# Recurrent layer of a twelve-layer network: a quarter of the product with B on GpSimd, step sizes computed once

## The reference, cut to what matters

```python
xz = x @ in_proj_w.T + in_proj_b
x_main, z = jnp.split(xz, 2, axis=-1)
xc = silu(causal_conv(x_main, conv_w) + conv_b)          # 4 taps, per channel
ssm = xc @ x_proj_w.T + x_proj_b                         # 33 columns
B_param, C_param = ssm[..., :16], ssm[..., 16:32]
delta = softplus(ssm[..., -1:])                          # one step size per position
A = -exp(A_log)                                          # 256 x 16
h = exp(A * dt) * h + dt * B_t * x_t                     # over 512 positions, per channel and state
y = sum over states of h * C_t + D * x_t
y = (y * silu(z)) @ out_proj_w.T + out_proj_b
out = layernorm(y + x) * gamma + beta
```

## Time and profile before

| | us |
|---|---|
| three timed runs | 2643.38, 2636.57, 2642.61 |
| their median | 2642.61 |
| profiled execution, its time | 2648.85 |
| its span, first to last instruction | 2647.0 |
| busy: TensorE, VectorE, ScalarE, GpSimd | 2102.6, 1704.8, 1021.6, 495.3 |
| mean granted TensorE clock, share of full speed | 0.867 |

### The profile page before, as it was taken

One profiled execution on the slowest core, in us unless ns is written; L12 is line 12 of the kernel. 1 busy time (PEld: TensorE's weight loads), 2 busy tenths in 40 slices (PEclk: granted clock), 3 DMA queues, 4 the chain that ended last, 5 costly groups with the idle time before them and its releaser, 6 DMA issues. The chain is left out here.

```text
span 2647.0 us, 35471 instructions
## 1 busy us (share of the span) xinstructions
PE 2102.6 (79%) x11888; PEld 1380.2 (52%) x11912; DVE 1704.8 (64%) x4085; ACT 1021.6 (39%) x2225; POOL 495.3 (19%) x843
## 2 busy tenths in 40 slices
PE   6696999976997895547774996597599869988788
PEld 3453888853554444112222454486333346766677
DVE  5565677764675556789997455456689665655655
ACT  2353222211564451444441343321177723443333
POOL 0331111001111420226662331010211000000000
PEclk8597999986897797679997798799699879999989
DMA  8320000003111310000001320001311010000000
GB/s 314 98 57 13 1 1 1 1 24 96 49 49 36 96 45 0 0 0 0 0 0 63 95 44 13 0 1 42 119 41 43 23 40 1 0 0 0 0 1 17
DMA packets 60046, 94.41 MB, mean 36 GB/s; under 512 B 11312, under 2 KB 33136, under 8 KB 58736
## 3 DMA queue, kind: packets, MB, share of 16 engines
q1 hardware_dynamic: 29792, 55.57, 6.2%
q0 software_dynamic: 29952, 36.45, 5.7%
q10 hardware_dynamic: 144, 0.39, 0.1%
HBM read 65.63 MB, written 31.29 MB: 37 GB/s over the span
## 5 line engine op out<-in xcount | busy, mean ns | idle before, releaser
L904 DVE TENSOR_REDUCE m<-banks 128x1 f32<-128x512 f32 (+3 forms) x512 | 272.6, 584 | 80.1 <-PE banks L1057 53.5
L2435 PEld LDWEIGHTS banks<-w_ffn,eh 128*128 128x128 f32 x2144 | 280.1, 191 | 21.7
L2435 PE MATMUL banks<-w_ffn,eh 128*128 128x128 f32 x2144 | 281.7, 275 | 0.0
L1325 DVE TENSOR_REDUCE m<-banks 128x2 f32<-128x308 f32 x384 | 164.3, 475 | 173.2 <-PE banks L1604 97.2
L1025 ACT ACTIVATE p<-banks 128x512 f32<-128x512 f32 (+3 forms) x512 | 233.7, 522 | 97.0 <-PE banks L1103 56.6
L2423 PE MATMUL banks<-x_hi,w_hi 128*128 128x512 f32 x472 | 211.7, 448 | 18.7 <-PEq L330 18.7
L1055 PE MATMUL banks<-K,Qf 32*128 32x512 f32 (+2 forms) x512 | 181.1, 511 | 38.1 <-PEq L330 33.2
L2425 PE MATMUL banks<-x_hi,w_lo 128*128 128x512 f32 x472 | 188.7, 400 | 0.0
L2424 PE MATMUL banks<-x_lo,w_hi 128*128 128x512 f32 x472 | 188.0, 398 | 0.0
L2405 ACT ACTIVATE et<-banks 128x512 f32<-128x512 f32 x140 | 83.7, 598 | 248.5 <-PE banks L2425 198.2
L2715 POOL TENSOR_TENSOR hc<-sh,cb 128x1024 f32<-128x1024 f32 x64 | 153.1, 2393 | 113.6 <-ACT cb L2730 108.0
(11 more groups left out here) (398 smaller groups left out, 4293.1 us busy)
## 6 DMA issues: line engine op xcount, KB each, us to landing
Qf<-stack_q_plain POOLq DMA_DIRECT2D x48, 256.0 KB, 3.0
Qf<-stack_q_masked POOLq DMA_DIRECT2D x32, 256.0 KB, 3.0
K<-stack_k_self POOLq DMA_DIRECT2D x32, 256.0 KB, 3.1
w_ffn<-ffn_dram SPq DMA_DIRECT2D x1, 6144.0 KB, 35.7
stack_q_plain<-q_hi SPq DMA_DIRECT2D x24, 256.0 KB, 3.5
stack_q_masked<-q_hi SPq DMA_DIRECT2D x16, 256.0 KB, 2.9
stack_k_self<-k_hi SPq DMA_DIRECT2D x16, 256.0 KB, 3.1
K<-stack_k_ctx POOLq DMA_DIRECT2D x48, 80.0 KB, 2.6
```

What stands on the lines that cost most here:

```text
L904: ins = dve.reduce_max(k.m[:, t, h:h + 1], bank[:, 0:(t + 1) * P if k.kind == "page" else S], AX)
L1325: dve.reduce_max(k.m[:, t:t + 2, h], first_banks[c % 3][:].rearrange("p (a k) -> p a k", a=2)[:, :, 0:S2], AX).then_inc(sem("max_done"), 1)
L2435: last = pe.matmul(bank[:, t * P:(t + 1) * P], k.h[:, n % RING, t * P:(t + 1) * P], w(down.format(e))[:, i * P:(i + 1) * P], start=(i == 0 ...
```

## The change

In the scan, VectorE makes only the first 384 of the 512 columns of each half of `dbx`. ScalarE copies the last 128 columns of B from PSUM to SBUF (`bb`), after its copy of C of the step before, and GpSimd multiplies `dtx` by that copy, ahead of its multiplication by C of the step before. VectorE now waits for the copy (`bb_ready`) before its part of `dbx`, and for GpSimd's part (`rest_dbx`) before the scans. `dtx` has two buffers and is made for the next batch at s = 8.

In the inputs, the step size argument is formed with the positions along the partitions: per batch four times two matmuls with `xc` as the stationary operand and one column of weights, all batches into 16 columns of one bank. B and C of batch b go to rows 32 b to 32 b + 31 of one bank. After the last batch, the softplus chain runs once on 128 x 16 and the split once on 128 x 512; ScalarE copies the parts to their places in `k.bc` (twelve copies of 32 x 512); VectorE makes diagonal matrices of the step sizes, TensorE multiplies them by a matrix of ones (16 matmuls of 128 x 128), and ScalarE copies the result to `k.dt`. The bodies of the removed `split`, `step_sizes` and `logarithms` (lines 2510 to 2535 and 2587 to 2593 of the kernel before) are left out:

```diff
--- before.py
+++ after.py
@@ -126,7 +126,7 @@
-    "m_xp_b": (1, lambda i: i["L2_attn_x_proj_b"][0:32].reshape(32, 1)),
+    "m_xp_b": (1, lambda i: np.tile(i["L2_attn_x_proj_b"][0:32].reshape(32, 1), (4, 1))),
@@ -2447,6 +2447,7 @@
+OWN = 384
@@ -2463,7 +2464,8 @@
-        self.dtx = sb("dtx", [P, 2, S])
+        self.dtx = sb("dtx", [P, 2, 2, S])
+        self.bb = sb("bb", [P, 2, S])
@@ -2478,17 +2480,19 @@
-    bf, bh = sb("bf", [32, S]), sb("bh", [32, S], BF16)
-    raw, e, ln, d, iz = (sb(name, [P, S]) for name in ("raw", "e", "ln", "d", "iz"))
+    bf, parts = sb("bf", [P, S]), sb("bparts", [P, 3, S], BF16)
+    raw, e, ln, d, iz, dt = (sb(name, [P, B * QT]) for name in ("raw", "e", "ln", "d", "iz", "dtp"))
+    diag = sb("diag", [P, 2, QT, P])
+    bc_bank, dt_bank = ps[4], ps[5]
-            dve.memset(k.bc[:], 0.0)
+            dve.memset(k.bc[96:P, :], 0.0)
@@ -2507,43 +2511,38 @@
-            def split(b):
...
-            def step_sizes(b):
...
             convolve(0)
...
             for b in range(B):
...
                 if b + 1 < B:
+                    convolve(b + 1)
+                activate(b)
+
+            dve.wait_ge(sem("dt_done"), B)
+            ch.link(dve.tensor_scalar(raw[:], dt_bank[:, 0:B * QT], w("m_dt_b"), None, ALU.add))
+            dve.scalar_tensor_tensor(e[:], raw[:], -1.0, raw[:], ALU.mult, ALU.max).then_inc(sem("abs_ready"), 1)
+
+            dve.wait_ge(sem("bc_done"), B)
+            ch.link(dve.tensor_scalar(bf[:], bc_bank[:], w("m_xp_b"), None, ALU.add))
+            for part in range(3):
+                dve.tensor_copy(parts[:, part], bf[:]).then_inc(sem("part_ready"), 1)
+                dve.wait_ge(sem("part_ready"), part + 1)
+                if part < 2:
+                    ch.link(dve.tensor_tensor(bf[:], bf[:], parts[:, part], ALU.subtract))
+
+            dve.wait_ge(sem("log_ready"), 1)
+            ch.link(dve.tensor_scalar(iz[:], d[:], -1.0, 0.0, ALU.add, ALU.is_equal))
+            ch.link(dve.scalar_tensor_tensor(d[:], d[:], -1.0, iz[:], ALU.add, ALU.add))
+            ch.link(dve.reciprocal(d[:], d[:]))
+            dve.tensor_tensor(ln[:], ln[:], iz[:], ALU.add)
+            ch.link(dve.tensor_tensor(d[:], d[:], e[:], ALU.mult))
+            ch.link(dve.tensor_tensor(d[:], d[:], ln[:], ALU.mult))
+            ch.link(dve.scalar_tensor_tensor(dt[:], raw[:], 0.0, d[:], ALU.max, ALU.add))
+            for b in range(B):
+                if b >= 2:
+
+                    dve.wait_ge(sem("spread_done"), b - 1)
+                dve.tensor_tensor(diag[:, b % 2], over(w("ident"), 1, QT), over(dt[:, b * QT:(b + 1) * QT], 2, P), ALU.mult).then_inc(sem("diag_ready"), 1)
+            dve.wait_ge(sem("diag_ready"), B)
@@ -2584,26 +2583,33 @@
-            def logarithms(b):
...
             act.wait_ge(sem("halved"), 1)
             first_tap(0)
...
             for b in range(B):
...
+                gate(b)
+                if b == 0:
+                    first_tap(1)
+                activate(b)
                 if b + 2 < B:
                     first_tap(b + 2)
+
+            act.wait_ge(sem("abs_ready"), 1)
+            nc.scalar.activation(e[:], e[:], ACT.Exp, scale=-1.0).then_inc(sem("e_ready"), 1)
+            act.wait_ge(sem("e_ready"), 1)
+            nc.scalar.activation(d[:], e[:], ACT.Identity, bias=1.0).then_inc(sem("e1_ready"), 1)
+            act.wait_ge(sem("e1_ready"), 1)
+            nc.scalar.activation(ln[:], d[:], ACT.Ln).then_inc(sem("log_ready"), 1)
+
+            for part in range(3):
+                act.wait_ge(sem("part_ready"), part + 1)
+                for b in range(B):
+                    last = nc.scalar.copy(k.bc[32 * part:32 * part + 32, b * S:(b + 1) * S], parts[32 * b:32 * b + 32, part])
+                last.then_inc(sem("part_placed"), 1)
+            for b in range(B):
+                act.wait_ge(sem("spread_done"), b + 1)
+                nc.scalar.copy(k.dt[:, b], ps[b][:]).then_inc(sem("dt_ready"), 1)
+            act.wait_ge(sem("dt_ready"), B)
+            act.wait_ge(sem("part_placed"), 3)
@@ -2618,20 +2624,30 @@
+            def parameters(b):
+                pe.wait_ge(sem("xc_ready"), b + 1)
+                for t in range(QT):
+                    for i in range(2):
+                        last = pe.matmul(dt_bank[:, b * QT + t:b * QT + t + 1], k.xc[:, b, i, t * P:(t + 1) * P], w("m_dt")[:, i * P:i * P + 1],
+                                         start=(b == 0 and t == 0 and i == 0), stop=(i == 1), skip_group_check=True)
+                last.then_inc(sem("dt_done"), 1)
+                for i in range(2):
+                    last = pe.matmul(bc_bank[32 * b:32 * b + 32, :], w("m_xp")[:, i * 32:(i + 1) * 32], k.xc[:, b, i], start=(i == 0), stop=(i == 1))
+                last.then_inc(sem("bc_done"), 1)
+
-                pe.wait_ge(sem("xc_ready"), b + 1)
-                if b >= 1:
-
-                    pe.wait_ge(sem("dt_ready"), b)
-                for i in range(2):
-                    last = pe.matmul(ps[5][:], w("m_dt")[:, i * P:(i + 1) * P], k.xc[:, b, i], start=(i == 0), stop=(i == 1))
-                last.then_inc(sem("dt_done"), 1)
-                for i in range(2):
-                    last = pe.matmul(ps[4][0:32, :], w("m_xp")[:, i * 32:(i + 1) * 32], k.xc[:, b, i], start=(i == 0), stop=(i == 1))
-                last.then_inc(sem("bc_done"), 1)
+                parameters(b)
+
+            pe.wait_ge(sem("xm_ready"), 2 * B)
+            pe.wait_ge(sem("z_ready"), 2 * B)
+            for b in range(B):
+                pe.wait_ge(sem("diag_ready"), b + 1)
+                for t in range(QT):
+                    last = pe.matmul(ps[b][:, t * P:(t + 1) * P], w("ones"), diag[:, b % 2, t, :], start=(t == 0), stop=True, skip_group_check=True)
+                last.then_inc(sem("spread_done"), 1)
@@ -2682,16 +2698,22 @@
                 xn = k.n.xn[:, e * QT:(e + 1) * QT, :]
                 dve.tensor_tensor(xn, out_bank[:].rearrange("p (t d) -> p t d", t=QT), xn, ALU.add).then_inc(sem("r_ready"), 1)
+            def weigh(e):
+                dve.tensor_tensor(k.dtx[:, e % 2], k.xc[:, e], over(k.dt[:, e], 1, 2), ALU.mult).then_inc(sem("dtx_ready"), 1)
+                dve.wait_ge(sem("dtx_ready"), e + 1)
+
+            weigh(0)
             for u in range(steps):
                 e, s = divmod(u, NSTATE)
-                if s == 0:
-                    ch.link(dve.tensor_tensor(k.dtx[:], k.xc[:, e], over(k.dt[:, e], 1, 2), ALU.mult))
-
-                dve.wait_ge(sem("B_done"), u + 1)
-                dve.tensor_tensor(k.dbx[:, u % 2], k.dtx[:], over(B_bank[:], 1, 2), ALU.mult).then_inc(sem("dbx_ready"), 1)
+                if s == 8 and e + 1 < B:
+                    weigh(e + 1)
+
+                dve.wait_ge(sem("bb_ready"), u + 1)
+                dve.tensor_tensor(k.dbx[:, u % 2, :, 0:OWN], k.dtx[:, e % 2, :, 0:OWN], over(B_bank[:, 0:OWN], 1, 2), ALU.mult).then_inc(sem("dbx_ready"), 1)
                 if e >= 1 and s == 1:
                     apply_gate(e - 1)
                 dve.wait_ge(sem("dbx_ready"), u + 1)
+                dve.wait_ge(sem("rest_dbx"), u + 1)
                 for i in range(2):
                     dve.wait_ge(sem("dA_ready"), 2 * u + i + 1)
                     if u >= 2 and i == 0:
@@ -2706,7 +2728,20 @@
         @block.gpsimd
         def _(pool):
+            def rest_dbx(u):
+                e, s = divmod(u, NSTATE)
+                if s == 0:
+                    pool.wait_ge(sem("dtx_ready"), e + 1)
+                pool.wait_ge(sem("bb_ready"), u + 1)
+                if u >= 2:
+
+                    pool.wait_ge(sem("h_ready"), 2 * u - 2)
+                nc.gpsimd.tensor_tensor(k.dbx[:, u % 2, :, OWN:S], k.dtx[:, e % 2, :, OWN:S], over(k.bb[:, u % 2, OWN:S], 1, 2), ALU.mult).then_inc(sem("rest_dbx"), 1)
+
+            rest_dbx(0)
             for u in range(steps):
+                if u + 1 < steps:
+                    rest_dbx(u + 1)
                 pool.wait_ge(sem("C_ready"), u + 1)
                 pool.wait_ge(sem("h_ready"), 2 * u + 2)
                 if u >= 2:
@@ -2716,6 +2751,14 @@
         @block.scalar
         def _(act):
+            def copy_B(u):
+                act.wait_ge(sem("B_done"), u + 1)
+                if u >= 2:
+
+                    act.wait_ge(sem("rest_dbx"), u - 1)
+                nc.scalar.copy(k.bb[:, u % 2, OWN:S], B_bank[:, OWN:S]).then_inc(sem("bb_ready"), 1)
+
+            copy_B(0)
             for u in range(steps):
                 e, s = divmod(u, NSTATE)
                 for i in range(2):
@@ -2728,6 +2771,8 @@
                 if u >= 2:
                     act.wait_ge(sem("hc_ready"), u - 1)
                 nc.scalar.copy(k.cb[:, u % 2], C_bank[:]).then_inc(sem("C_ready"), 1)
+                if u + 1 < steps:
+                    copy_B(u + 1)
         @block.tensor
         def _(pe):
```

More of the change, by code:

```diff
@@ L2537, in _ @@
             convolve(0)
-            activate(0)
-            convolve(1)
             for b in range(B):
```

(15 more changed lines are left out.)

## The result

The changed kernel takes 2624.45 us (median of 15 runs, 2608.73 to 2633.37) against 2647.38 us (15 runs of before beside them, 2636.28 to 2657.32): ratio 0.9899, 95% interval 0.9883 to 0.9915, or 22 to 31 us of 2647. The profiled execution took 2624.98 us, 23.9 less than that of before. One of the four timed runs of experiment 5 took 5505 us, twice as long as the others and for a reason that stays open; its ratio is that of the other three.

The account below looks back on a forecast made before the run. VectorE was taken to bound the scan, and a chain over three engines the changed inputs. Gains of 11 us (16.4 - 3.7 - 1.4) and 10.7 sum to 22: profiled 2648.85 to 2627, less 6.2 for the median, 2621 us; range 2604 to 2634.

Parts of the forecast that it names:

- The step of the scan: Scan: dbx falls by 0.257 to 0.937 us, a step from 3.48 to 3.22; 16.4 us over 64 steps.
- GpSimd's pace: Scan: 2.35 + 0.73 + 2 x 0.08 = 3.24 us a step, practically VectorE's 3.22; no loss taken.
- rival 1: Scan: GpSimd sets the pace, 6 to 10 us of the gain go, 2627 to 2631 us; chance 0.20.
- The stalls: Batch starts in the scan: VectorE's 1.94 us wait for B grows; four places by 0.92, 3.7 us lost.
- The gate waits: Step 1 of a batch in the scan: gate comes too early without dtx ahead; 3 x 0.45 = 1.4 us lost.
- The inputs: Block of scan_inputs: a chain over three engines orders it; 10.7 us gained, bounds 5 and 25.
- A round: Inputs, twice: parameters, projection, first tap, convolution with GpSimd in its way, activation; 20.0 us from one batch's xc to the next.
- The tail: End of the inputs, after the last m_xp: split, step sizes, diagonals, spread (7.1 us), last copy; from 1136.5 to 1149.8.
- GpSimd and VectorE excluding each other: GpSimd locks out VectorE operations with two SBUF inputs: convolve 6.43 against 4.32 us; charged in inputs, nothing in the scan.
- rival 2: Inputs gain more: TensorE keeps its upper level in parameters and spread, block 25 us shorter, 2607 us; chance 0.15.
- Rival 4: No measurable change: inputs block stays as long and GpSimd sets the scan's pace; 4 us left, 2639 us; chance 0.09.
- Rival 3: Slower: GpSimd's new scan operation costs over 1.25 us; 64 steps and some 6 us reach 247 us; chance 0.06.

Follow-up runs that it names:

- experiment 5: Changed kernel with TensorE's output product of a batch cut into four column blocks at s = 1, 3, 5, 7, residual at s = 9; ratio to before 0.9856.
- experiment 6: Changed kernel with GpSimd's two gate operations per batch in the inputs replaced by one of VectorE after activate(b); ratio to before 0.9888.
- experiment 3: Changed kernel with VectorE making 256 of 512 columns of dbx instead of 384, GpSimd the other 256; ratio to before 0.9969.
- experiment 10: Changed kernel with the two m_xp matmuls ahead of the eight one-column matmuls in parameters; ratio to before 0.9934.

## Why the prediction was right

**The sum.** 2621 us forecast, 2624.45 measured; a gain of 22 us against one of 22.9 in the medians. That the two gains are so close is partly luck: the stages gained 26.7 us, 4.7 more than forecast, and the rest of the kernel, which nobody changed, gave about 3 of that back in the profiled execution. What was right is the mechanism of each stage, as follows.

**The step of the scan.** 0.937 forecast for dbx, 0.931 measured; 3.22 for the step, 3.22 measured. The wait for GpSimd ahead of the scan cost nothing, as priced.

**GpSimd's pace.** Its operation was taken at 0.73 and is 0.728. The 0.08 us between two operations did not carry over: I read it from a pair where the second needs the first's result, and such pairs show it again in the changed kernel's inputs (end 1077.74, next start 1077.82). Between operations that don't depend on one another the next starts 0.05 us before the recorded end, so GpSimd's pace is 2.30 + 0.73 = 3.03, not 3.24, and VectorE leads by 0.18 us. The rule of the Trainium skill (Perfetto Trace Analysis, GPSIMD Engine Instruction), to go by starts and not by spans, holds here: 2.30 from start to start against a span of 2.35. The error in the sum was nil, since I had given GpSimd the pauses to catch up; but rival 1, with a fifth of the chance, drew on that row ("3.24 against 3.22 is already level"), and its own conditions, 0.88 us for the operation or 0.2 us between two, did not come true either. I had put GpSimd's busy share of the scan at over 90%; it is 86% (194.44 of 226): it waits 9.5 us for the scans and 22.3 us for ScalarE's copies (13.9 and 8.4).

**The stalls.** 1.94 + 0.92 = 2.86 forecast, 2.77 measured three times and one of 1.30 at the start; idle time ahead of dbx 6.0 before, 9.7 after, the 3.7 of the forecast. Experiment 5 shows the cause that I had argued. The gate waits 0.50 us in each of three batches, as forecast (0.45), but in the kernel before, these waits were not all zero, one of the three was 0.97: gated's idle time is 5.5 in the earlier trace rows (4.55 of it at the end), 6.1 after. I charged 1.4, and 0.5 was lost. With that, the 12.6 us instead of 11 are explained to about half a microsecond.

**The inputs.** The chain was right in kind and in order; four of its terms were off. To `xc` of batch 0: 20.5 us forecast from the block's start, 19.4 measured. A round: 20.0 forecast, 21.0 and 20.8 measured. The terms written down for it make only 19.5, so 0.5 of the 20.0 has no source; in their place parameters took 7.1 (6.85 forecast), projection and first tap 4.4 (3.6), GpSimd in the convolution 4.1 (3.5). From `xc` of batch 2 to the last m_xp: 13.8 forecast, 10.7 measured, because TensorE was at its upper level in the last parameters (3.8 us in place of 6.85). The tail: 13.3 forecast, 12.2 measured, the spread of the diagonals 5.7 us, partly at the upper level, in place of 7.1. So the size of the inputs' gain, 14.1 instead of 10.7, is the term "TensorE at the lower level throughout" in the last 20 us; experiment 6 shows the same records at 7.0 us, and there that stretch is 13.6 us, close to the forecast.

**GpSimd and VectorE excluding each other.** Charged in the inputs and not in the scan. Both are shown: 8.41 against 4.31 with GpSimd's two operations taken away (experiment 6), and `hc` of 2.35 us beside `dbx` and the scans, but 3.19 where it meets `dtx`, whose inputs both lie in SBUF. The lock that the Trainium skill states (SBUF, "Two separate sides") agrees with all three.

**The rivals.** The gain was not larger for a clock that kept its upper level (rival 2), though part of it came that way. Rival 4, no change, is excluded by the interval of 22 to 31 us. Rival 3 was priced too simply: experiment 3 shows that a scan with GpSimd ahead ends not at 64 paces plus 6 us but some 18 us above them even without its end.

## What to carry to other kernels

When work is handed to a second engine, compute that engine's own pace, start to start, between operations that don't depend on each other, and stop short of the point where it passes the first: here that lay between 160 and 256 of 512 columns, and beyond it the gain was gone (experiment 3). Look next at who stands ahead in the queue of the engine that makes the shared operand: spreading a 4 us piece of work over four steps gave 8.4 us, and a different order of two calls in the inputs 13.6, a third and a half of what the change itself gained. A long stretch of little work on VectorE is not yet a short stage; of 33 us of work taken out of the inputs 14 arrived, and the order in TensorE's queue held back another 13.6.

## What was not expected of the hardware

The same twenty matmul records in the same place of TensorE's queue took 3.8 us in one kernel and 7.0 in another, with a granted clock of 1.00 and 0.50, and in experiment 10 the clock rose after one of two like stretches. So in this block, where TensorE works in bursts, a stage's length was uncertain by about 3 us for that reason alone, and the end of the scan by 2. And GpSimd and VectorE slow each other both ways: the two GpSimd operations, 4.75 us by themselves, added 4.1 us to each convolution and were themselves stretched to about 2.8 and 2.67.
